# The next chunk's low-rank input products issued ahead of the narrow tail tile's down products, in a macaron block on one core

## What is computed

```python
for e in range(NUM_EXPERTS):
    c = jnp.sum(jnp.where(sf == e, wf, 0.0), axis=1)
    lo_up = LORA_ALPHA * (xt @ up_A[e].T @ up_B[e].T)
    lo_gate = LORA_ALPHA * (xt @ gate_A[e].T @ gate_B[e].T)
    h_e = jax.nn.silu(base_up + lo_up) * (base_gate + lo_gate)
    ch = c[:, None] * h_e
    mixed_h = mixed_h + ch
    lora_down = lora_down + LORA_ALPHA * (ch @ down_A[e].T @ down_B[e].T)
out = mixed_h @ w_down.T + lora_down
...
x = x + 0.5 * _L0_ffn_ref(_layernorm(x, axis=-1), ...)
x = x + _L0_attn_ref(_layernorm(x, axis=-1), ...)
x = x + 0.5 * _L0_ffn_ref(_layernorm(x, axis=-1), ...)
```

## Time and profile before

| | |
|---|---|
| median of 3 runs | 1544.28 us (1543.22 to 1545.04) |
| the profiled execution | 1547.47 us, of which the span in the profile is 1545.7 us |
| mean granted clock of TensorE | 0.987 of full speed |
| busy: PE, DVE, ACT, POOL | 1450.9, 1148.4, 945.3, 807.8 us |
| chunk 1 (g = 1), from 102.2 us | 59.6 us |
| chunk 2, from 161.8 us (eight more transposes, a loop turn) | 60.9 us |
| chunks 5 and 6 (loop turns), from 1358.4 us | 59.3 us each |

### The profile page before, as it was taken

The page is one execution under the profiler, slowest core; times in us unless marked ns, Lnnn a source line. Parts: engine busy times, 40 slices in busy tenths (PEclk is TensorE's granted clock), DMA queues, the critical chain, the costliest instruction groups (busy, mean ns, idle before and its releaser), DMA issues.

```text
span 1545.7 us, 26680 instructions
## 1 busy us (share of the span) xinstructions
PE 1450.9 (94%) x8992; PEld 1280.4 (83%) x8992; DVE 1148.4 (74%) x2536; ACT 945.3 (61%) x1951; POOL 807.8 (52%) x735
## 2 busy tenths in 40 slices
PE   5799999789999999999999999999999976999998
PEld 4578777679899899989989998998999865877776
DVE  7678878877776777777677767767767776787787
ACT  4444444577776777677677767767767644444443
POOL 4546345355556555555555555555555543633644
PEclk9899999999999999999999999999999998999999
DMA  4000000200000000000000000000000020000000
GB/s 164 1 0 1 1 0 0 68 8 8 15 8 8 15 8 8 15 1 15 15 1 8 21 1 8 22 1 8 8 1 1 9 102 0 1 15 0 14 14 14
DMA packets 10822, 23.55 MB, mean 15 GB/s; under 512 B 848, under 2 KB 4944, under 8 KB 10576
## 3 DMA queue, kind: packets, MB, share of 16 engines
q1 hardware_dynamic: 10704, 22.04, 4.2%
HBM read 19.94 MB, written 2.10 MB: 14 GB/s over the span
## 4 chain that ended last, share of the span: by engine, by line
PE 78%; DVE 12%; issue 5%; POOL 2%; ACT 1%; DVEq 0%; DMA 0%; POOLq 0%; ACTq 0%
PE ps L1184 23%; PE ps L1186 22%; PE ps L1185 22%; PE ps L1475 9%; DVE ps L1114 2%; DVE up_act L971 1%; DVE pT_l L310 1%; POOL w_l L310 1%; DVE hid L981 1%; DVE hid L986 1%; DVE x_sb L915 1%; DVE xn L836 1%; DVE base_gate L956 1%; ACT up_act L661 0%; DVE stats L817 0%
## 5 line engine op out<-in xcount | busy, mean ns | idle before, releaser
L582 POOL TENSOR_SCALAR probs<-probs,inv_sum 128x128 f32<-128x128 f32 (+7 forms) x256 | 210.6, 823 | 390.8 <-DVE inv_sum L1070 390.7
L1114 DVE CUSTOM_DVE_ANT_0 ps<-ps,causal 128x128 f32<-128x128 f32 (+7 forms) x256 | 195.1, 762 | 217.6 <-PE ps L1186 216.0
L764 ACT ACTIVATE probs<-ps,neg_max 128x128 f32<-128x128 f32 (+7 forms) x256 | 189.3, 740 | 76.2 <-DVE neg_max L1114 76.2
L310 DVE TENSOR_TENSOR pT_l<-ps,pT_h 128x512 fp32r<-128x512 f32 (+3 forms) x384 | 200.8, 550 | 2.1 <-ACT pT_h L743 1.9
L743 ACT ACTIVATE pT_h<-ps 128x512 fp32r<-128x512 f32 (+3 forms) x384 | 174.1, 490 | 37.6 <-PE ps L1475 35.1
L571 POOL TENSOR_TENSOR rot_sin<-swapped,rope 128x512 f32<-128x512 f32 x128 | 165.0, 1289 | 55.5 <-ACT swapped L720 52.5
L1475 PE MATMUL ps<-ident,probs 128*128 128x128 f32 x1152 | 169.8, 274 | 23.3 <-DVE pT_l L310 20.4
L1184 PE MATMUL ps<-pT_h,v_h 128*128 128x256 f32 x640 | 181.1, 283 | 0.8 <-DVE oA_l L310 0.8
L1186 PE MATMUL ps<-pT_h,v_l 128*128 128x256 f32 x640 | 180.9, 283 | 0.0
L1185 PE MATMUL ps<-pT_l,v_h 128*128 128x256 f32 x640 | 180.6, 282 | 0.0
L310 POOL TENSOR_TENSOR hid_l<-hid,hid_h 128x512 fp32r<-128x512 f32 (+1 forms) x88 | 114.1, 1297 | 98.1 <-ACT hid_h L663 98.1
(11 more groups left out here) (185 smaller groups left out, 4336.4 us busy)
## 6 DMA issues: line engine op xcount, KB each, us to landing
w_raw<-attn_w SPq DMA_DIRECT2D x32, 256.0 KB, 2.6
w_in<-ffn_w SPq DMA_DIRECT2D x10, 744.0 KB, 9.1
x_sb<-x_in SPq DMA_DIRECT2D x4, 512.0 KB, 5.4
out<-x_sb SPq DMA_DIRECT2D x4, 512.0 KB, 2.9
rope<-rope_w SPq DMA_DIRECT2D x1, 1024.0 KB, 7.9
expand_raw<-expand_w SPq DMA_DIRECT2D x2, 384.0 KB, 12.4
```

What stands on the lines that cost most here:

```text
L310: return eng.tensor_tensor(dst, src, high.bitcast(F32), ALU.subtract)
L582: pool.tensor_scalar(probs[s % 4][:, 0:n], probs[s % 4][:, 0:n], inv_sum[:, s % 4:s % 4 + 1], 1.0, ALU.mult, ALU.mult).then_inc(probs_read ...
L764: act.activation(probs[t % 4][:, 0:a * n].rearrange("p (a n) -> p a n", a=a), view, ACT.Exp, bias=neg_max[:, t % 4:t % 4 + 1], scale=-1.0, ...
L1114: dve.tensor_tensor_reduce(out=view, in0=view, in1=causal[:, SEQ - a * n:].rearrange("p (a n) -> p a n", a=a), scale=-SCALE, scalar=HUGE, ...
```

## The change

The low-rank input products of a chunk leave the head of the chunk. For the first chunk of a pass they are issued in `ffn`, as before. For each other chunk they are issued in the chunk before it, between `down(4)` and `down_a(5, 0)`, with both halves together. In chunks 2 and 3 `turn_before` then stands alone at the head. On PE, ACT, DVE and POOL the hardware loop over the chunks is replaced by a loop of the host program, so that all eight chunks are written out.

```diff
-                with pe.Fori(2 - f, CHUNKS) as c:
+                for c in range(2 - f, CHUNKS):
                     ffn_chunk(c + 4 * f, c, f, False, f == 0)
...
                 if first:
                     base(BG, FULL)
-                else:
-                    low_rank_products(g, c, (0,))
-                    if turns:
-                        turn_before(c + 2, g)
-                    low_rank_products(g, c, (1,))
+                elif turns:
+                    turn_before(c + 2, g)
                 pe.wait_ge(cm_padded, g + 1)
...
                 down(HT - 3).then_inc(mixed_used, 1)
                 down(HT - 2)
+                if c < CHUNKS - 1:
+                    low_rank_products(g + 1, c + 1)
                 down_a(HT - 1, 0)
                 down_a(HT - 1, 1).then_inc(down_a_done, 1)
                 down(HT - 1)
```

More of the change, by code:

```diff
@@ L563, in ffn @@
                     ffn_chunk(1, 1, f, False)
-                with pool.Fori(2 - f, CHUNKS) as c:
+                for c in range(2 - f, CHUNKS):
                     ffn_chunk(c + 4 * f, c, f, False)
@@ L697, in ffn @@
                     ffn_chunk(1, 1, f, False)
-                with act.Fori(2 - f, CHUNKS) as c:
+                for c in range(2 - f, CHUNKS):
                     ffn_chunk(c + 4 * f, c, f, False, f == 0)
@@ L1036, in ffn @@
                     ffn_chunk(1, 1, f, False)
-                with dve.Fori(2 - f, CHUNKS) as c:
+                for c in range(2 - f, CHUNKS):
                     ffn_chunk(c + 4 * f, c, f, False, f == 0)
```

## The result

The changed kernel takes 1553.75 us in the median of six runs (1550.65 to 1557.22), the kernel before 1544.66 us in six. The ratio is 1.0061, with an interval of 1.005 to 1.0072: slower by about 9 us (7.7 to 11.1). Forecast were 1550.5 us and a range up to 1553.5. The direction was right; the size was a third short, and the median lies 0.25 us outside the range.

A forecast was written before the change was run, and what follows sets the result against it. PE, busy for 94% of the span, was taken as the bound. Waits of 3.8 us and clock falls of 2.4 us took the profiled 1547.47 us to 1553.7; runs lie 3.2 us lower, so 1550.5 us, range 1546.5 to 1553.5.

The forecast's parts named there:

- The late `cm_pad`: Heads of chunks 1, 5, 6, 7: late `down_a_done` delays the mask copy, transposes 0.93 to 1.28 us late, +4.4 us.
- waits alone: All chunk boundaries: 4.4 us late starts plus 0.2 us slow first transposes minus 0.8 us at turned heads, +3.8 us.
- The clock: Behind new waits at four heads: granted clock falls at about two, 1.2 us each, +2.4 us, bounds 0 and 6.
- The reason given for fewer falls: Heads with new waits: six base matmuls run directly behind the transposes, so the trace doesn't decide whether the clock falls.
- the starting point: Whole kernel before the change: the shown runs' 1544.28 us, 3.2 us below the profiled execution's 1547.47 us.
- The form of the loop: Steady chunks on PE: 59.6 us written out, 59.3 us as a loop turn, so neither form shows a cost.
- rival (c): Chunk loops: writing them out gives back the waits' cost, 1 us in all, no clock fall; 1547.1 us, 17 in 100.
- rival d: Chunk tails: filled waits count, late `cm_pad` doesn't; some 8.5 us faster, 1536 us, 4 in 100.

The follow-up runs named there:

- e2_fill: Changed kernel with six base gate products issued twice at heads of chunks 1, 5, 6, 7, first ahead of the `cm_pad` wait; 1549.43 us, 1.0023 to before.
- r1_changed: The changed kernel run once more without edit, on one chip with the written-out kernel; 1553.77 us, ratio 1.0059 to the kernel before.
- e4_cm_early: Changed kernel with DVE's copy of the next mask into `cm_pad` moved ahead of its wait for `down_a_done`; 1543.51 us, ratio 0.9981 to before.
- e6_behind: Changed kernel with the twelve low-rank products issued behind the `down_a` pair but ahead of `down(5)`; 1545.25 us, ratio 1.0 to before.
- e5_half_early: Changed kernel with only the up half of the low-rank products moved and `cm_pad` copied ahead of DVE's `down_a_done` wait; 1536.18 us, ratio 0.9945 to before.
- e7_mask_ahead: Changed kernel with the next mask's transposes also in the tail, its rounding and `cm_pad` copy earlier; 1536.76 us, ratio 0.9945 to before.
- e3_half: Changed kernel with only the up half of the low-rank products moved, the gate half at the next head; 1540.38 us, ratio 0.9961 to before.
- r3_behind: Changed kernel with low-rank products behind the `down_a` pair, run again on one chip with the written-out kernel; 1545.18 us, ratio 0.9999 to before.

## Why the prediction was right in its chain and short in its size

- **The late `cm_pad`: right, in place and size.** At the boundaries from chunk 0 to 1 and from 4 to 5 the transposes were forecast 1.28 and 1.26 us late and are 1.29 and 1.27 us late. Forecast were 3.8 us of waits alone; e2_fill, whose late `cm_pad` is the same and has no fall of the clock behind it, is 3.6 us slower than before (2.0 to 4.9). That these totals meet so closely is in part luck: e2_fill also had a somewhat higher mean clock than the kernel before on the same chip (0.988 against 0.986, over 11 and 28 runs). By chunks: chunks 5 and 6 were forecast 0.99 and 1.03 us longer and are 0.86 and 0.89 in e2_fill. That chunk 1 gets shorter by the turned head of chunk 2 was forecast as 0.39 us and is 0.21 (0.32 in r1_changed, where the clock did not fall in chunk 1); chunk 2 0.45 and 0.55. Early copying of `cm_pad` (e4_cm_early) and late low-rank products (e6_behind) each take the loss away, so it hangs on this one chain.
- **The clock: the step that failed.** The prediction put the term as "a fall at about two of the four places, at 1.2 us each", 2.4 us, with bounds of 0 and 6. The size of one fall was right: 0.9 to 1.3 us from head to head. The count was not: four in one profile and three in the other, seven of eight. From the profiles of the changed kernel and e2_fill the term is 4.3 us (0.93 + 1.26 + 1.14 in chunks 1, 5 and 6, and 0.97 in chunk 7 up to L1003), from the medians' ratios 5.9 us. The mean granted clocks of all runs agree: 0.983 and 0.982 in the two sets of six runs of the changed kernel, 0.988 in the eleven of e2_fill, 0.988 and 0.987 in those of the written-out kernel. The reason given for fewer falls, six base matmuls directly behind the transposes, did not hold: in the first profile the clock fell while these six ran, and in the second, at three heads, already with the first of the transposes ahead of them, before any of the six had begun. With four falls at 1.2 us the same sum would have given 1552.9 us. Another 0.4 us of the distance is the starting point: the kernel before has a median of 1544.66 us over six runs, and the forecast started from 1544.28 over three.
- **The form of the loop: wrong, and small.** That "neither the loop nor the written-out form shows a cost on PE" came from comparing chunk 1 with chunk 5, which differ in more than the loop; chunk 2 against chunk 1 would have been the comparison, and from head to head it was 0.4 us longer. Two runs give 3.3 and 2.2 us for the written-out loops. In the chunks whose tail the moved products fill most of this gain is not to be expected, since they cover the wait in which 0.3 of the 0.5 us lie; that is worked out and no run was made for it. So it offsets less of the loss than rival (c) asked for: PE's wait at the head of chunk 5 is as long as in chunk 1 (2.22 us in both).
- **Faster by 8.5 us, if `cm_pad` were not late (rival d).** It ranked lowest and was ruled out by the lengths of the two chains, 3.7 and 1.5 us. An early `cm_pad` was needed but was not the whole condition: in e4_cm_early it is early with all twelve moved, and PE waits 0.9 us for the low part of the mask instead. In e5_half_early and e7_mask_ahead that wait is gone too, and they are 8.5 us faster than before. But 2.2 to 3.3 us of that come from the written-out loops, so by difference the filled waits are worth 5 to 6 us, not 8.5.

## What to carry to other kernels

Work that is moved into one wait leaves a place where it covered another; ask what chain ran beneath it there, and where in that chain the moved work now stands. Here twelve matmuls filled 1.0 us, sat in front of the two products that a 3.5 us chain on DVE starts from, and uncovered that chain. Take what the next head needs out of that chain first (one copy of 0.22 us was enough to undo the loss), or move only as much as the wait holds. And where PE gets a new wait of some 2 us in otherwise dense work, count the clock's fall behind it as likely, not as an even chance.

## What the runs showed of the hardware

- One wait of 2.2 us in dense matmuls was followed by the granted clock at 0.50, the 1.2 GHz level, in seven of eight cases in two profiles, for about 3 us. Waits of 1.16 us in the turned heads and of 0.81 to 0.85 us in e3_half and e2_fill were followed by none. A wait shorter than 2.2 us is no safe mark elsewhere: at the head of chunk 4 of the changed kernel waits of 1.09 and 1.41 us stand 2 us apart, and the clock fell there too. The Trainium skill, "TensorE: Matmul & The Clock Gate", Part 1, says that the monitor runs free of the kernel's start so that counts differ between runs; the case of chunk 1, with a fall in one profile (61.17 us) and without in the other (60.13 us), agrees.
- Spare matmuls can be worth their time: 24 of them, issued into four waits, made the kernel 4.3 us (medians) to 5.9 us (ratios) faster.
- Between the attention and pass 1, in a stretch that the change doesn't touch, the profiles are of two kinds. From the first `wk_h` product behind pass 0 to the head of chunk 4 it is 1006.5 to 1007.9 us in eight of them and 1009.0 to 1009.3 in four (both of the changed kernel, e4_cm_early and e6_behind). The four are those in which the clock falls once more, behind PE's wait of 1.5 us for `w_l` at the start of pass 1. All twelve have this wait. Windows behind it, of the changed kernel and of the kernel before:

```profile
1289.50:1292.80 3.30, 3.30 (x8) 2.62 (x9) 2.52 (x35) 0.00 (x0) 0.00 (x0) 0.51 0.01 2
1287.30:1290.60 3.30, 3.30 (x14) 2.48 (x14) 2.53 (x35) 1.21 (x3) 0.00 (x0) 1.00 0.00 0
```

  It goes by the run and not by the kernel: r3_behind is the kernel of e6_behind, and its profile has no such fall.
- Over all runs the mean granted clock is 0.986 in e4_cm_early and in both sets of e6_behind, against 0.988 and 0.987 in the written-out kernel. By the changed kernel and e2_fill, where 0.005 of mean clock went with 4.3 to 5.9 us, that is worth 1.5 to 2.5 us, an estimate. It is most of the 2 to 3 us by which these two came out above what their chunks say. Why their clock is lower stays open.
